# A decoder layer on one core: inverse roots of the layer norms as a power on POOL

## The reference

```
def _layernorm(x, axis=-1, eps=1e-05):
    m = jnp.mean(x, axis=axis, keepdims=True)
    v = jnp.var(x, axis=axis, keepdims=True)
    return (x - m) / jnp.sqrt(v + eps)

x = _layernorm(x + attention(x))                  # latent attention, 16 heads, causal, RMS norms inside
x = _layernorm(x + cross_attention(x, ctx_512))   # 16 heads of 32, causal
x = _layernorm(x + ffn(x))                        # shared experts and 16 routed ones, top 2, exact Gelu
```

## Time and profile before

| what | value |
|---|---|
| time, median of 3 executions | 901.39 us (900.47 to 902.63) |
| the profiled execution: its own time | 902.72 us |
| the profiled execution: its span | 900.9 us |
| PE busy in the span | 838.2 us, 93% |
| DVE | 528.1 us, 59% |
| ACT | 474.8 us, 53% |
| POOL | 240.8 us, 27% |
| mean granted clock of TensorE | 0.988 |

### The profile page before, as it was taken

One profiled execution on the slowest core, in us unless ns is written; L12 is line 12 of the kernel. 1 busy time (PEld: TensorE's weight loads), 2 busy tenths in 40 slices (PEclk: granted clock), 3 DMA queues, 4 the chain that ended last, 5 costly groups with the idle time before them and its releaser, 6 DMA issues.

```text
span 900.9 us, 13299 instructions
## 1 busy us (share of the span) xinstructions
PE 838.2 (93%) x4302; PEld 710.2 (79%) x4302; DVE 528.1 (59%) x979; ACT 474.8 (53%) x1225; POOL 240.8 (27%) x278
## 2 busy tenths in 40 slices
PE   6978999999999987889998789999999999999997
PEld 5766888788788775777776678888888988889896
DVE  3553753654664557666767755636465665656467
ACT  5514752743753554676576651525473745637150
POOL 0222230132132021455455100431232332321420
PEclk9989999999999998999999999999999999999999
DMA  8022315133322400321222020543464564653432
GB/s 324 1 78 63 123 43 157 65 99 98 123 85 55 146 21 21 84 49 38 55 52 67 2 71 24 183 166 119 146 206 164 187 199 153 198 166 131 137 94 82
DMA packets 39486, 96.33 MB, mean 107 GB/s; under 512 B 15824, under 2 KB 21840, under 8 KB 37808
## 3 DMA queue, kind: packets, MB, share of 16 engines
q1 hardware_dynamic: 28384, 57.95, 20.6%
q0 software_dynamic: 11056, 37.79, 12.9%
HBM read 71.59 MB, written 20.97 MB: 103 GB/s over the span
## 4 chain that ended last, share of the span: by engine, by line
PE 62%; issue 15%; DVE 8%; ACT 7%; POOL 4%; SPq 1%; DMA 1%; POOLq 0%; ACTq 0%; DVEq 0%
PE ps L1490 50%; ACT Pt L829 3%; PE ps L1505 3%; PE ps L1830 2%; POOL Pt L593 2%; PE ps L1820 1%; PE ps L1550 1%; PE ps L1640 1%; DVE negmax L1101 1%; SPq L514 1%; DVE acc L1117 1%; PE ps L1711 1%; PE ps L1832 1%; DVE kb L1218 1%; DVE stats L1123 1%
## 5 line engine op out<-in xcount | busy, mean ns | idle before, releaser
L593 POOL TENSOR_TENSOR Pt<-Pt,rowinv 112x448 f32<-112x448 f32 x64 | 59.9, 936 | 226.6 <-DVE rowinv L1108 226.2
L829 ACT ACTIVATE Pt<-ps,negmax 112x112 f32<-112x112 f32 x256 | 87.2, 356 | 49.1 <-DVE negmax L1101 49.0
L1490 PE MATMUL ps<-x2T_hi,ws_hi 128*128 128x448 f32 x256 | 96.0, 375 | 4.3 <-DVE x2T_lo L1030 4.3
L1490 PE MATMUL ps<-x2T_lo,ws_hi 128*128 128x448 f32 x256 | 94.2, 368 | 0.0
L1490 PE MATMUL ps<-x2T_hi,ws_lo 128*128 128x448 f32 x256 | 94.1, 368 | 0.0
L1490 PE MATMUL ps<-w_hi,h_hi 128*128 128x512 f32 x224 | 89.9, 401 | 0.0
L957 ACT ACTIVATE hf<-ps,b 128x448 f32<-128x448 f32 x64 | 40.6, 635 | 92.3 <-PE ps L1490 72.9
L1490 PE MATMUL ps<-w_hi,h_lo 128*128 128x512 f32 x224 | 88.5, 395 | 0.0
L1490 PE MATMUL ps<-w_lo,h_hi 128*128 128x512 f32 x224 | 88.4, 395 | 0.0
L1030 DVE TENSOR_TENSOR h_lo<-hf,h_hi 128x448 fp32r<-128x448 f32 x64 | 39.9, 623 | 48.7 <-ACT h_hi L958 47.9
L1374 DVE TENSOR_TENSOR acc<-ps,acc 128x512 f32<-128x512 f32 x56 | 38.6, 689 | 44.4 <-PE ps L1490 35.4
(11 more groups left out here) (282 smaller groups left out, 2248.6 us busy)
## 6 DMA issues: line engine op xcount, KB each, us to landing
stage<-in_wf SPq DMA_DIRECT2D x30, 513.0 KB
rows_in<-in_zeros SPq DMA_DIRECT2D x30, 256.0 KB, 4.0
xs<-rows_in POOLq DMA_DIRECT2D x29, 256.0 KB, 4.3
rows_out<-yb POOLq DMA_DIRECT2D x29, 256.0 KB
stage<-in_wa SPq DMA_DIRECT2D x4, 1408.0 KB, 6.6
stage<-in_wb SPq DMA_DIRECT2D x4, 1280.0 KB, 5.6
qr<-ro_hi SPq DMA_DIRECT2D x64, 56.0 KB, 2.0
qr<-ro_lo SPq DMA_DIRECT2D x64, 56.0 KB, 2.0
```

The costliest lines, as they stand in the source:

```text
L593: nc.gpsimd.tensor_tensor(p, p, rowinv[0:S, b % 2, :].unsqueeze(2).broadcast_to([S, GH, S]), ALU.mult).then_inc(norm_done, 1)
L829: last = nc.scalar.activation(Pt[0:S, b % 2, h * S:(h + 1) * S], ps[0:S, b % 2, h * S:(h + 1) * S], ACT.Exp, bias=negmax[0:S, b % 2, h:h + 1],
L1490: ins = mm(dst, w, x, start=start and i == 0, stop=stop and i == len(ops) - 1, skip_group_check=not (start and stop))
```

## The change

The square roots on ACT and the reciprocals on DVE go. In their place POOL raises `rstd` to the power -0.5 in one TENSOR_TENSOR instruction for each part, with a 128x1 tile `minus_half`, broadcast, as exponent. It waits for `ln_eps` and signals `ln_inv`, for which DVE waits as before. The steps SQRT and EXP, the tile `warm` and the semaphore `ln_root` go too. In POOL's lists the power stands behind the last work of the attention (ATT_LAST_POOL), in the cross attention between the splits of batches 5 and 6 for part 0 and at the end for part 1 (X_LAST_POOL), and for the last norm behind the gathers of the FFN. The diff, cut:

```diff
 ATT_LAST_ACT = weave(range(8), _act, fill={
     **_last, 5: [("G", 7), ("CX",)], 6: [("L",)],
-    7: [("K", 0), ("SQRT",), ("ROOT1", 0), ("ROW1", 0), ("ROW1", 1)]}) + [
-    ("Z", 6), ("T", 7), ("U1", 0), ("U1", 1), ("Z", 7), ("U1", 2), ("U1", 3), ("ROOT1", 1), ("V", 0),
-    ("ROW1", 4), ("ROW1", 5), ("ROOT1", 2), ("EXP",), ("ROW1", 6)]
+    7: [("K", 0), ("ROW1", 0), ("ROW1", 1)]}) + [
+    ("Z", 6), ("T", 7), ("U1", 0), ("U1", 1), ("Z", 7), ("U1", 2), ("U1", 3), ("V", 0),
+    ("ROW1", 4), ("ROW1", 5), ("ROW1", 6)]
...
-ATT_LAST_POOL = weave(range(8), _pool, fill={5: [("CX",)], 6: [("LK",)], 7: [("L",)]})
+ATT_LAST_POOL = weave(range(8), _pool, fill={5: [("CX",)], 6: [("LK",)], 7: [("L",), ("ROOT1", 0)]}) + [
+    ("ROOT1", 1), ("ROOT1", 2)]
...
 X_LAST_ACT = [
     ("S", 4), ("Z", 1), ("T", 3), ("X",), ("S", 5), ("T", 4), ("S", 6), ("Z", 3), ("T", 5), ("S", 7), ("Z", 4),
-    ("T", 6), ("Z", 5), ("SQRT",), ("T", 7), ("ROOT2", 0), ("Z", 6), ("ROW2", 0), ("ROW2", 1), ("Z", 7), ("U2", 0),
-    ("U2", 1), ("U2", 2), ("U2", 3), ("ROOT2", 1), ("ROW2", 4), ("ROW2", 5), ("ROW2", 6), ("FF", 0), ("U2", 4),
+    ("T", 6), ("Z", 5), ("T", 7), ("Z", 6), ("ROW2", 0), ("ROW2", 1), ("Z", 7), ("U2", 0),
+    ("U2", 1), ("U2", 2), ("U2", 3), ("ROW2", 4), ("ROW2", 5), ("ROW2", 6), ("FF", 0), ("U2", 4),
     ("FF", 1), ("U2", 5), ("U2", 6), ("FF", 2), ("FF", 3)]
...
-X_LAST_POOL = [("N", 4), ("Z", 1), ("X",), ("N", 5), ("N", 6), ("Z", 3), ("N", 7), ("Z", 4), ("Z", 5), ("Z", 6),
-               ("Z", 7)]
+X_LAST_POOL = [("N", 4), ("Z", 1), ("X",), ("N", 5), ("N", 6), ("Z", 3), ("N", 7), ("Z", 4), ("Z", 5), ("ROOT2", 0),
+               ("Z", 6), ("Z", 7), ("ROOT2", 1)]
...
+            def inverse_roots(lo, hi, part):
+
+                pool.wait_ge(ln_eps, part + 1)
+                nc.gpsimd.tensor_tensor(rstd[:, lo:hi], rstd[:, lo:hi], minus_half[:, :].broadcast_to([P, hi - lo]),
+                                        ALU.pow).then_inc(ln_inv, 1)
...
+            nc.gpsimd.memset(minus_half[:, :], -0.5).then_inc(one_set, 1)
             nc.gpsimd.memset(one[:, :], 1.0).then_inc(one_set, 1)
-            pool.wait_ge(one_set, 1)
+            pool.wait_ge(one_set, 2)
...
+            for t in range(TT):
+                inverse_roots(t, t + 1, LN_ALL + t)
...
-            def layernorm_root(i, r):
-                lo, hi = LN_PARTS[i][r]
-                act.wait_ge(ln_eps, ln_part(i, r) + 1)
-                nc.scalar.activation(rstd[:, lo:hi], rstd[:, lo:hi], ACT.Sqrt).then_inc(ln_root, 1)
-
...
-            def function_ready(func):
-                nc.scalar.activation(warm[:, :], one[:, :], func)
...
-            for t in range(TT):
-                act.wait_ge(ln_eps, LN_ALL + t + 1)
-                nc.scalar.activation(rstd[:, t:t + 1], rstd[:, t:t + 1], ACT.Sqrt).then_inc(ln_root, 1)
-
...
             def inverse_roots(i, r):
                 lo, hi = LN_PARTS[i][r]
                 part = ln_part(i, r) + 1
-                dve.wait_ge(ln_root, part)
-                nc.vector.reciprocal(rstd[:, lo:hi], rstd[:, lo:hi]).then_inc(ln_inv, 1)
                 dve.wait_ge(ln_inv, part)
...
                 V.tensor_scalar(rstd[:, t:t + 1], mv[:, t, 1:2], LN_EPS, None, ALU.add).then_inc(ln_eps, 1)
-                dve.wait_ge(ln_root, LN_ALL + t + 1)
-                V.reciprocal(rstd[:, t:t + 1], rstd[:, t:t + 1]).then_inc(ln_inv, 1)
                 dve.wait_ge(ln_inv, LN_ALL + t + 1)
```

More of the change, by code:

```diff
@@ L298, in build @@
         one = sb("one", [P, 1])
-        warm = sb("warm", [P, 1])
+        minus_half = sb("minus_half", [P, 1])
         minus = sb("minus", [P, TT])
@@ L450, in build @@
             "pt_free z_done z_hi z_free rot_add rot_hi rot_lo").split())
-        (ln_stat, ln_mv, ln_eps, ln_root, ln_inv, ln_minus, ln_row, ln_out, lt_done, lt_hi, lt_lo) = map(sem, (
-            "ln_stat ln_mv ln_eps ln_root ln_inv ln_minus ln_row ln_out lt_done lt_hi lt_lo").split())
+        (ln_stat, ln_mv, ln_eps, ln_inv, ln_minus, ln_row, ln_out, lt_done, lt_hi, lt_lo) = map(sem, (
+            "ln_stat ln_mv ln_eps ln_inv ln_minus ln_row ln_out lt_done lt_hi lt_lo").split())
         kb_zero, cxs_hi, cxs_lo, zs_hi, zs_lo = map(sem, "kb_zero cxs_hi cxs_lo zs_hi zs_lo".split())
@@ L653, in att_step @@
                     low_l(0)
+                elif kind == "ROOT1":
+                    inverse_roots(*LN_PARTS[0][j], ln_part(0, j))
             turns(pool.Fori, AJ, ATT_POOL_PRE, ATT_POOL, ATT_LAST_POOL, att_step)
@@ L694, in x_step @@
                     low_l(g)
+                elif kind == "ROOT2":
+                    inverse_roots(*LN_PARTS[1][j], ln_part(1, j))
                 elif kind == "F":
@@ L760, in _ @@
                 act.sem_inc(s_, n)
-            act.wait_ge(one_set, 1)
+            act.wait_ge(one_set, 2)
             for k in range(KD):
@@ L887, in att_step @@
                     split_l(0)
-                elif kind == "ROOT1":
-                    layernorm_root(0, j)
                 elif kind == "ROW1":
                     row(0, j)
[L892 to L895, removed]
                 elif kind == "U1":
@@ L934, in x_step @@
                     turned(0, j, x1T_hi)
-                elif kind == "ROOT1":
-                    layernorm_root(0, j)
                 elif kind == "ROW1":
                     row(0, j)
-                elif kind == "ROOT2":
-                    layernorm_root(1, j)
                 elif kind == "ROW2":
                     row(1, j)
-                elif kind == "SQRT":
-                    function_ready(ACT.Sqrt)
                 elif kind == "U2":
```

## The result

The changed kernel takes 907.63 us (median of 5; 906.55 to 909.66) against 901.34 us for the kernel before in the same comparison: a ratio of 1.0071, 95% interval 1.0053 to 1.0088. It is slower by 6.3 us, where a gain of 1.2 us was forecast. The range of the forecast ended at 905.7.

What follows compares the result with a forecast made beforehand. TensorE was taken as the bound almost everywhere, so norms count only where it stands still. Terms -0.04+1.07+0.2-0.11+0.08 gave 1.20 us, so 901.39-1.20 = 900.2 us, range 899.2 to 905.7.

Steps and rivals of the forecast that it cites:

- The price of a power: POOL's power of n columns: estimated 0.2 us plus 0.1 a column, upper bound 0.5 a column.
- First norm, tiles 0 to 3: Wait from rstd's end to minus goes from 0.65 to 0.69 us, a loss of 0.04; POOL's hold on DVE unchanged.
- Tiles 4 and 5: First norm: nothing counted, as DVE waits 0.53 us for a matmul, covering the 0.4 us power.
- Tile 6: First norm: table load leaves the path, rstd to row 6 falls from 1.65 to 0.58 us, gain 1.07.
- rival (d): Tile 6's gain is absorbed by POOL's DMA wait or the key DMAs; 0.13 us stay, 901.3; chance 0.07.
- rival (a): Power nearly free, TensorE keeps its clock from 370 to 374; gain 2.1 us, time 899.3; chance 0.20.
- Second norm: Tiles 0 to 3 gain 0.2 us, power hidden beside DVE's jobs; tiles 4 to 6 lose 0.11.
- The sum up to the last norm: First and second norm terms together: -0.04+1.07+0.2-0.11 us.
- Last norm: Seven tiles: only the last gains, 0.08 us; TensorE keeps setting the 3.03 us period.
- Rival (b): POOL's power becomes the wait in every norm, above all the last seven tiles; up to 905.7; chance 0.24.
- (c): First power, first norm tiles 0 to 3, slow from cold code; measurably slower from 3.0 us; chance 0.04.
- The step that failed: Last norm: powers stand last in POOL's queue, behind gathers already issued; no cost was counted for this.

Runs made afterwards that it cites:

- e9: Kernel before, roots still on ACT, with POOL's query-weight subtraction held until DVE's two first-norm rows are done; 898.99 us against 901.80, ratio 0.9971.
- e1: Changed kernel with the last norm's seven roots given back to ACT and DVE; 901.64 us against 902.09, ratio 0.9995.
- e3b: Kernel before plus only a wait for the last tile's variance at the end of POOL's program, no instruction behind it; 907.19 us, ratio 1.0059.

## Why the prediction was wrong, point by point

**The price of a power.** Estimate 0.2+0.1n us, bounds 0.2 and 0.2+0.5n; measured 0.39+0.16n. The price of a column was within the bounds; the base was taken from the 128x2 multiplication, and a power's is twice that. The hand-overs, 0.07 and 0.02 us, held: rstd ends at 368.0, the power starts at 368.05, ends at 368.60, and minus starts at 368.64.

**First norm, tiles 0 to 3.** Forecast a loss of 0.04. The changed kernel's rows:

```profile
350.62 1.98 DVE L1123 TENSOR_SCALAR rstd<-mv 128x4 f32<-128x4 f32 x1
...
353.74 0.16 DVE L1130 SCALAR_TENSOR_TENSOR minus<-mv,rstd 128x4 f32<-128x4 f32 x1 [0.62 <-POOL rstd L617]
...
354.81 1.82 PE L1563 MATMUL ps<-ident,acc 128*128 128x128 f32 x8 [2.60 <-ACT acc L819]
```

rstd ends at 352.60 and minus starts at 353.74: 1.14 us instead of 0.65, a loss of 0.49. The term was mis-sized by the price of the power, 1.03 us for 0.6. TensorE waited 2.60 us where it had waited 2.08. The hold by POOL was read rightly, but as a fixed thing; it was the larger matter (e9).

**Tiles 4 and 5.** Right: DVE still waits for TensorE behind them, 0.39 us, though the power took 0.71 us where 0.4 was assumed.

**Tile 6.** Forecast 1.07 us gained. The changed kernel's rows:

```profile
367.82 0.15 DVE L1123 TENSOR_SCALAR rstd<-mv 128x1 f32<-128x1 f32 x1
...
368.05 0.55 POOL L617 TENSOR_TENSOR rstd<-rstd,minus_half 128x1 f32<-128x1 f32 x1 [3.09 <-DVE rstd L1123]
...
368.64 0.16 DVE L1130 SCALAR_TENSOR_TENSOR minus<-mv,rstd 128x1 f32<-128x1 f32 x1 [0.66 <-POOL rstd L617]
...
368.83 0.81 ACT L819 ACTIVATE acc<-acc,minus,rstd 128x512 f32<-128x512 f32 x1 [2.11 <-DVE minus L1130]
...
370.88 0.37 PE L1528 MATMUL ps<-maskb,identb 112*112 112x448 bf16 x1 [1.76 <-DVE qx_lo L1023]
```

From the end of rstd (367.97) to row 6 it is 0.86 us instead of 1.65: 0.79 gained, less by the power's price. TensorE waits 1.76 us instead of 2.51. The gain was not absorbed, as rival (d) had it. What rival (a) said of the clock came true here: the stretch from 370 to 374 has it at 1.00, where rows 12 have 0.65.

```profile
370.00:374.00 4.00, 3.12 (x23) 1.00 0.57 178
```

In all seven kernels here with the powers in the first two norms TensorE waits 1.70 to 1.76 us at this place and the clock behind it is 1.00; in the five with roots on ACT it waits 2.51 to 2.54, and the clock is 0.61 to 0.66 in four and 1.00 in e9. Of the table loads four are gone, 12 to 8, as forecast.

**Second norm.** Tiles 0 to 3: right in its mechanism, the power (499.24 to 500.26) ran beside DVE's two jobs, and minus followed them at once, at 500.31. TensorE's wait for row 0 fell from 0.93 to 0.59 us. But nothing of it was left at rstd for tiles 4 to 6, 10.61 us after that for tiles 0 to 3 where it had been 10.56, because the clock fell behind this shorter wait. Windows from 501 to 505, the kernel before and the changed one:

```profile
501.00:505.00 4.00, 3.02 (x22) 1.00 0.00 0
```

```profile
501.00:505.00 4.00, 3.57 (x15) 0.62 0.01 2
```

So it did in five of the seven kernels with the powers, and in one of the five without. In the two that kept it (six tiles on POOL, and the added drain) the same stretch takes 10.22 us: 0.34 gained, the shorter wait. The sum had no term for that; rival (a) names it as what speaks against it. Tiles 4 to 6: from the end of rstd (509.77) to minus (510.74) 0.97 us instead of 0.48, a loss of 0.49 where 0.11 was forecast.

**The sum up to the last norm** is therefore 0.79+0.2-0.49-0.49 = 0, where 1.12 was forecast. The trace shows 0.4 us gained (519.0 to 518.6), with the clock kept at tile 6 and lost in the second norm. e1, which is this part alone, measures no change. This half of the forecast was right in its waits and too high by 0.7 us in size.

**Last norm.** The period stayed at 3.03 us and the last tile's wait grew from 0.47 to 0.66 us. Rival (b), that DVE sets the pace there, didn't come about: it needed 0.57 us a power, and it was 0.55. I had the right sign of the result only in cases (b) and (c), and both for the wrong reason. No mechanism I named was the one that acted.

**The step that failed** is the sentence "POOL's gathers are all issued by then, and the powers stand last in its queue". It was meant to show that the powers hold nobody. But an instruction at the very end of POOL's queue moves the start of POOL's closing drain. The drain was 8.2 us long, and before the change it was done 22.5 us before SP was; after it, SP waits 5.6 us for it. The sum put this term at nothing. The forecast asked for what stands behind the power on POOL and counted only the program's own instructions. The row was there in the trace of before, under the line of the block: a drain of 9475 ns at 868.7. (Two marks of rival (b) are a little off by its own rows: its total turns negative at about k = 0.23, not 0.25, and passes 1.8 us at about 0.37. Nothing hangs on them; k came out at 0.16, with a base of 0.39 instead of 0.2.)

## What to carry to other kernels

Before an instruction is put at the end of an engine's program, ask what that engine does after its last instruction, and how much slack there is to the end: if POOL has issued many DMAs, its closing drain took some 0.07 to 0.08 us for each here, so POOL should be through that much before the last store has landed, or be given an explicit drain where time is free. Look for it in the instructions of the block's own line and in the waits of the queue that ends last; the timeline of busy engines doesn't show it. An instruction of DVE that takes ten times its usual time and ends together with one of POOL's was a hold here, and the cure was to move POOL's instruction past the whole chain of DVE's, not past the first one of it.

## What the runs showed of the hardware that was not expected

- POOL's closing drain: 0.16 us without DMAs of its own, 0.25 with one, 2.80 with 32, 8.15 with 115; the same for plain DMAs and gathers, and not less although DVE had used what the last of them brought 21 us before (the kernel with the wait alone). A second drain a little later costs next to nothing: 0.65 us with a power of 0.54 in it. The Trainium skill (VectorE: DVE Perf Modes, The DRAIN you can't avoid) gives about 12 ns, on all five engines, for the drains of a kernel's preamble and postamble. SP's at the block's end has that size with 13 ns, POOL's hasn't, and for these the measurement decides.
- A power on POOL, 0.39+0.16n us for n columns on 128 partitions, with no slow first instance and no load of code to be seen in the rows.
- The clock behind a wait of TensorE is not given by the length of that wait. At the first norm it stayed at 1.00 behind 1.25 and 1.36 us and fell behind 2.07 to 2.60 us in nine of ten traces (to 0.50 to 0.84), but not in e3b, which waits 2.08. In the second norm it fell behind 0.59 us more often than behind 0.93. What else decides is not shown.
